# One more column in 128 fetched row by row on SyncE and ScalarE, and the passes written out

## The reference, cut to what matters

```python
def gcn_conv(x, src, dst, W, b, n_nodes):
    ...
    msg = h[src] * norm[:, None]
    out = jax.ops.segment_sum(msg, dst, num_segments=n_nodes)
    return out + b
def _edgeconv(x, src, dst, tw, tb, pw, pb):
    phi = x @ pw.T + pb
    diff = x[src] - x[dst]
    msg = diff @ tw.T + tb + phi[dst]
    agg = jax.ops.segment_max(msg, dst, num_segments=x.shape[0])
```

## Time and profile before

| | |
|---|---|
| median of 3 runs | 8914.77 us (8910.58 to 8919.87) |
| the profiled execution | 8913.79 us |
| its span, first to last instruction | 8912.1 us |
| PE busy | 7402.8 us (83%) |
| DVE busy | 5602.8 us (63%) |
| ACT busy | 823.6 us (9%) |
| POOL busy | 6615.4 us (74%) |

### The profile page before, as it was taken

How to read it: one execution, slowest core, us unless ns; L and a number is a source line. 1 busy time by engine, 2 the same in 40 slices (tenths; PEclk the granted TensorE clock), 3 DMA queues, 4 the chain that set the end, 5 groups by cost and what they waited for, 6 DMA issues and landing times. The chain is left out here.

```text
span 8912.1 us, 149042 instructions
## 1 busy us (share of the span) xinstructions
PE 7402.8 (83%) x34933; PEld 4053.7 (45%) x35458; DVE 5602.8 (63%) x11977; ACT 823.6 (9%) x2271; POOL 6615.4 (74%) x6356
## 2 busy tenths in 40 slices
PE   5999658887886899959997899959995899959994
PEld 2444347777775344434443344434443344434442
DVE  6777534444444777657775776757775776657775
ACT  3000011111113100010000100010001100010000
POOL 5777768888884677777777777777776777777777
PEclk8999867777777999979998999979997999979997
DMA  6555635555555333333333333333334333343334
GB/s 236 180 177 181 191 80 79 75 77 77 77 77 105 105 118 118 118 111 119 118 118 120 110 118 117 114 117 118 118 118 142 109 117 118 117 125 118 118 118 143
DMA packets 645241, 1072.25 MB, mean 120 GB/s; under 512 B 159799, under 2 KB 485007, under 8 KB 590297
## 3 DMA queue, kind: packets, MB, share of 16 engines
q0 software_dynamic: 295648, 412.64, 22.1%
q1 hardware_dynamic: 335527, 652.35, 21.3%
q10 hardware_dynamic: 13692, 3.78, 0.2%
HBM read 514.18 MB, written 562.58 MB: 121 GB/s over the span
## 5 line engine op out<-in xcount | busy, mean ns | idle before, releaser
L1056 POOL DMA_INDIRECT WORK<-table,stage x5040 | 4826.7, 958 | 1752.2 <-issue 1476.3
L1224 PE MATMUL bank<-TF,XF 128*128 128x512 bf16 x16800 | 5127.5, 386 | 485.8 <-DVE TF L1162 462.9
L1224 PE MATMUL bank<-TF,Z 128*128 128x512 bf16 x8400 | 3235.3, 385 | 4.8
L1224 PEld LDWEIGHTS bank<-TF,XF 128*128 128x128 bf16 x17150 | 1687.2, 99 | 2547.9 <-DVE TF L1162 329.5
L1162 DVE TENSOR_TENSOR TF<-AF,bank 128x3584 bf16<-128x3584 bf16 x1225 | 2470.7, 2017 | 314.0 <-PE bank L1224 308.2
L1189 DVE SCALAR_TENSOR_TENSOR WORK<-WORK,RESET 128x128 f32<-128x128 f32 x2928 | 1031.3, 352 | 892.4 <-DMA WORK<-table,stage 513.1
L1406 POOL DMA_INDIRECT acc<-TOT,stage x832 | 1296.0, 1558 | 275.7 <-issue 197.5
L1224 PEld LDWEIGHTS bank<-TF,Z 128*128 128x128 bf16 x8575 | 850.7, 99 | 1047.9 <-issue 64.2
L1189 DVE SCALAR_TENSOR_TENSOR WORK<-WORK,KEEP 128x128 f32<-128x128 f32 x2196 | 774.2, 353 | 663.2 <-DMA WORK<-table,stage 360.1
L1611 DVE SCALAR_TENSOR_TENSOR BASE<-bank,WEIGHT,BASE 128x128 f32<-128x128 f32 x832 | 234.3, 344 | 764.0 <-PE bank L1481 762.9
L1087 ACT COPY TOT<-bank 128x512 f32<-128x512 f32 x175 | 102.6, 586 | 5939.9 <-PE bank L1224 5539.5
(11 more groups left out here) (259 smaller groups left out, 3296.5 us busy)
## 6 DMA issues: line engine op xcount, KB each, us to landing
run_rows<-WORK SPq DMA_DIRECT2D x357, 1024.0 KB
WORK<-table ACTq DMA_DIRECT2D x5376, 0.5 KB
WORK<-table SPq DMA_DIRECT2D x5376, 0.5 KB
WORK<-table,stage POOLq DMA_INDIRECT x5040, 3.7
fill_rows<-BASE SPq DMA_DIRECT2D x52, 1024.0 KB
WORK<-fill_rows SPq DMA_DIRECT2D x104, 512.0 KB, 3.7
AF<-src_keys SPq DMA_DIRECT2D x175, 128.0 KB
table<-TF SPq DMA_DIRECT2D x56, 384.0 KB
```

Of the source, the lines that this page charges most:

```text
L1056: pool.indirect_dma_start(RUN[:, b, k, :], None, table, table_row(table, stage[:, b, k:k + 1]))\
L1224: i = nc.tensor.matmul(bank(2 + h)[:, 0:BATCH], PIECES[n][:, c * PART + k, :], OHOT[:, ((h + 1) * CHUNKS + c) % 2, k, :], start=c + k + n ...
```

## The change

`REGS` goes from 16 to 32: a part is one register load and 32 single rows, on both engines. `single(it, h)` says which columns come so: column 15 of the first half in rounds 1 to 12, as before, and now also column 15 of the second half (column 47) in odd rounds; GpSimd skips these. A column is four parts, two on SyncE and two on ScalarE. The semaphores and the row numbers are kept apart for the two halves. The registers are allocated once and not per pass. All `Fori` loops of a pass but TensorE's are replaced by Python loops, so that the code is written out and offsets and wait values are constants; `hold` becomes `wait`.

```diff
-SHARE = P // 2
-REGS = 16
+REGS = 32
+SHARE = 2 * REGS
...
+        def single(it, h):
+            return 0 < it < ROUNDS and (h == 0 or it % 2 == 1)
...
+            def alone(eng, regs, it, h, first, s):
+                if first % SHARE == 0:
+                    eng.wait_ge(solo_in[h], 16 * singles(it, h))
+                    eng.wait_ge(stored[2 * h], 16 * it)
+                    eng.wait_ge(reduced, (it - 1) * SPAN + h * COLS + HALF + 1)
+                eng.reg_load(regs, SOLO_I[0:1, h, first:first + REGS])
+                for k in range(REGS):
+                    row = eng.snap(regs[k], min_val=0, max_val=N_PAD - 1)
+                    eng.dma_start(RUN[first + k:first + k + 1, 2 * h, SOLO, :], table[ds(row, 1), :]).then_inc(s, 16)
...
-                        if (j % COLS >= OWN or j == SOLO) and not (first and j < COLS):
+                        if j % COLS >= OWN and not (first and j < COLS):
+                            continue
+                        if j % COLS == SOLO and single(it, j // COLS):
                             continue
...
# ScalarE, in each half round h after the copy and the indices:
-                        if not last:
-                            solo(it, h)
+                        if h == 0:
+                            solo(it, 1, 1)
+                            solo(it + 1, 0, 0)
+                        elif not last:
+                            solo(it + 1, 0, 1)
+                            solo(it + 1, 1, 0)
...
# SyncE, after the store of chunk b:
-                        if not last:
-                            solo(it, b)
+                        if b % 2 == 0:
+                            load_single(it + 1, b // 2)
+                        if b == 0:
+                            solo(it, 1, 1)
+                        else:
+                            solo(it + 1, b // 3, (b - 1) % 2)
...
# the same on SyncE, GpSimd and ScalarE:
-                body(0)
-                sp.addr_align(256, max_nops=8)
-                with sp.Fori(1, ROUNDS - 1) as it:
-                    body(it)
-                body(ROUNDS - 1, last=True)
+                for it in range(ROUNDS):
+                    body(it, last=it == ROUNDS - 1)
```

More of the change, by code:

```diff
@@ L313, in gnn_kernel @@
         added = [sem(f"added{k}", phase=False) for k in range(ACCS)]
+        regs_s = [nc.sync.alloc_register(f"row_sp{k}") for k in range(REGS)]
+        regs_a = [nc.scalar.alloc_register(f"row_act{k}") for k in range(REGS)]
         assert cleared[-1].num - cleared[0].num + 1 == len(cleared)
@@ L1012, in _, with singles @@
                     sp.wait_ge(x_saved, 16 * NG)
+        def single(it, h):
+            return 0 < it < ROUNDS and (h == 0 or it % 2 == 1)
+        def singles(it, h):
+            return sum(single(r, h) for r in range(it + 1))
         def turns(k):
             if k == SOLO:
-                return T // COLS - (ROUNDS - 1)
+                return T // COLS - sum(singles(ROUNDS - 1, h) for h in range(2))
             return T // COLS if k < OWN else 1
@@ L1076, in carry_clear @@
                     .then_inc(patched, 16)
-                hold(pool, patched, pbase + 32)
+                wait(pool, patched, pbase + 32)
             def act_part(act):
@@ L1081, in indices @@
                     wait(act, reduced, (c - BUFS + 1) * HALF)
[L1082 removed]
+                    act.copy(stage[:, b, :], SRCF[:, c * HALF:(c + 1) * HALF]).then_inc(staged, 1)
                 def rows_out(m, h):
@@ L1087, in rows_out, with solo @@
                     act.copy(TOT[:, h, 0:BATCH], bank(2 + h)[:, 0:BATCH]).then_inc(e_copied, 1)
[L1089 to L1099, removed]
+                def solo(it, h, part):
+                    if single(it, h):
+                        alone(act, regs_a, it, h, SHARE + part * REGS, solo_act[h])
                 def mixed(it, first=False, last=False):
@@ L1125, in act_part @@
                         i.then_inc(split_mid, 1)
[L1126 to L1131, removed]
+                solo(1, 0, 0)
+                for it in range(ROUNDS):
+                    mixed(it, first=it == 0, last=it == ROUNDS - 1)
             def dve_part(dve, st):
@@ L1247, in store @@
                 def store(c, b, first, n):
-                    hold(sp, reduced, c * HALF + first + n)
+                    wait(sp, reduced, c * HALF + first + n)
                     sp.dma_start(run_view[:, ds((c * HALF + first) * F, n * F)],
@@ L1253, in load_keys, with load_single, solo @@
                 def load_keys(m, h):
-                    hold(sp, onehot, (m - 2) * CHUNKS)
+                    wait(sp, onehot, (m - 2) * CHUNKS)
                     sp.dma_start(EKEYS_I[:, h, :], src_keys[ds((m * COLS + OWN) * P, BATCH)]
                                  .rearrange("(a n) -> a n", a=1).to_broadcast([P, BATCH])).then_inc(keys_in[h], 16)
[L1258 to L1270, removed]
+                def load_single(it, h):
+                    if single(it, h):
+                        sp.dma_start(SOLO_I[:, h, :], solo_rows[it * 2 + h:it * 2 + h + 1, :]).then_inc(solo_in[h], 16)
+                def solo(it, h, part):
+                    if single(it, h):
+                        alone(sp, regs_s, it, h, part * REGS, solo_sp[h])
                 def restore(g):
@@ L1284, in body @@
                         if fill:
-                            hold(sp, reduced, c * HALF + HALF // 2)
+                            wait(sp, reduced, c * HALF + HALF // 2)
                             sp.dma_start(fill_view[:, ds(c * HALF * F, HALF * F)], blank)\
@@ L1306, in sp_part @@
                     restore(0)
-                hold(sp, patched, pbase + 16)
+                wait(sp, patched, pbase + 16)
                 for g in range(NG):
```

32 lines of the change are left out of this document (13 added, 19 removed).

## The result

The changed kernel takes **9204.12 us** in the median of 4 runs (9198.03 to 9213.81); the kernel before, beside it, 8912.67 us (8906.75 to 8919.87). The ratio is 1.0327, with a 95% interval from 1.0315 to 1.0339. The forecast was 8862 us, in 8845 to 8900: the sign was wrong, and the distance is 342 us. The profiled execution took 9199.2 us, with a span of 9197.5.

What follows compares the result with a forecast made beforehand. POOL's gathers, at 1.263 us each, were taken to bound the kernel. 8913.8 us less 53.0 for 42 saved gathers gave 8860.8, or 8862 on the median, with everything else at nothing; range 8845 to 8900.

Steps and rivals of the forecast that it cites:

- the gathers saved: On POOL, 714 gathers a pass instead of 720, 42 fewer in seven passes at 1.263 us each: 53.0 us less.
- the code: Writing the loops out was costed at nothing, with bounds of 0 to 10 us either way.
- The loop: SyncE's and DVE's cycle over two rounds, closed by the late keys: 133.3 us, 4.4 shorter than POOL's 137.7.
- A part, 17.1 us: On SyncE, store, one register load and 32 single rows, 16.8 us, taken as 17.1; six stand in two rounds.
- the low end: A load of 32 registers was taken to cost no more than one of 16, so 0 us extra.
- The range's other end: Load of 32 registers in proportion: another 1.23 us, or another 2.87 if what stands behind the store doubled too.
- From the keys to the store, 30.7 us: Keys landing 2.5 us, then DVE's 28 columns at PE's pace, 28.2 us, to the store of chunk 1.
- rival 3: No change: PE's stalls and lowered clock at late keys make 139 us per two rounds, 8915 us in all; chance 0.06.
- The slack, 20 us: POOL has 27 gathers left on average, 34 us, against DVE's 14 us: about 20 us of lateness cost nothing.
- Rival 1: SyncE becomes the bound, slower: passes lengthen from 18.6 us per part; with 20.0, 52 us a pass, 9275; chance 0.12.
- the second: Rival: DVE and PE lateness just over the slack, up to 5 us of POOL wait a pass, 8880 to 8897; chance 0.11.
- the signs of being wrong: POOL waiting for DVE over 0.3 us, a load near 6 us, SyncE never idle through a pass, stores over a chunk late.

Runs made afterwards that it cites:

- the run meant for it: Changed kernel with 28 rows per part on SyncE and 36 on ScalarE, keys still behind the part: 9571.04 us, 1.0735 of the kernel before.
- the other: Changed kernel with SyncE's register load issued ahead of the chunk's store, keys still behind the single rows: 12404.28 us, 1.0124 of the kernel before.

## Why the prediction was wrong

**The bound, the gathers saved, the code.** Right. POOL bounded the passes, 42 gathers at the same beat are gone, and where nothing holds POOL up the pass lasts 902.4 us, as said. With the keys ahead and the first pass eased, which gives six of the 42 gathers back (7.6 us), the sum of the prediction is 8870 and the kernel takes 8868.47 (the kernel before took 8917.91 beside it, 3 more than in the sum); so the written-out code and the traffic together are worth some us at most, inside the 0 to 10 given for the code.

**The loop.** The mechanism was seen: the keys behind six parts are "what is late next". The ring was summed to 133.3 us, 4.4 under POOL's 137.7; it measured 145.6. The step that failed is this sum and the slack set against it. Three sizes in it were wrong:

- *A part, 17.1 us.* Six of them up to the late keys were put at 102.6 and took 110.9, 8.3 us of the 12.3. Most of that is the load of 32 registers, for which the prediction took "the low end", as for 16. Its line after, beside the earlier trace rows:

```profile
L1045 ACTq TENSOR_LOAD <-rowb x252: 2119/2143/6283, 187.6 to 9020.0; - x126
L1045 SPq TENSOR_LOAD <-rowb x252: 3797/4022/6429, 201.4 to 9036.9; - x126
```

  On ScalarE 2143 ns against 1292, so 53 ns for each further register; on SyncE behind a store 4022 against 2872, 1.15 us a part and 6.9 a ring. The argument "like one round trip and not like 16" was wrong: more registers take longer, though not in proportion. The range's other end had +1.23, which is nearly what came on SyncE. By itself it would not have turned the forecast: 133.3 + 6.9 = 140.2 is 2.5 over POOL's 137.7, 15 us in six double rounds, inside the 20 of slack that I set against it.
- *From the keys to the store, 30.7 us.* Measured 34.8 (3333.75 to 3368.52), the other 4.1. The landing is 3.3 us and not 2.5, and DVE's 28 columns take 31.5 and not 28.2. After the stop PE stands too, for 5.03 us, and only starts at 3339.14, once the first compare (2.02 us) is done. Then it starts slowly. By window (busy us of PE, PEld, DVE, ACT, POOL, then granted clock, DMA, GB/s):

```profile
3340.00:3345.00 5.00, 5.00 (x14) 1.82 (x13) 3.91 (x7) 0.00 (x0) 3.78 (x5) 0.55 0.18 51
3345.00:3350.00 5.00, 5.00 (x27) 2.55 (x26) 3.16 (x5) 0.00 (x0) 0.30 (x1) 1.00 0.04 15
```

  The granted clock was 1.00 until PE stood, 0.55 from 3340 to 3345 (near the lower of its two levels, 1.2 GHz), and 1.00 again after. Until 3344.2 three matmuls together took 1.28 us where they took 0.65 before the stop. DVE's third and fourth compare after the stop waited 2.17 and 1.29 us for PE, where the later ones wait 0.83 to 0.88. The prediction priced this clock only under rival 3, as PE's own time; it belongs in the ring, behind the late keys.
- *The slack, 20 us.* It is about 12.6. I counted the gathers that POOL has left on average. But the stop is at column 3 of a half round, and when POOL asks at the start of the next chunk, it has only this chunk's 12 gathers (15.1 us) less about 2.5 for the three columns. This figure is worked out afterwards, and no run varied it. The timeline shows POOL wait at such starts already in round 2, and again at the start of round 4:

```profile
3205.34 0.95 POOL L1074 DMA_INDIRECT WORK<-table,stage  x1 [2.04 <-DVE WORK L1200]
...
3311.28 0.95 POOL L1074 DMA_INDIRECT WORK<-table,stage  x1 [1.96 <-DVE WORK L1200]
```

With the three sizes in place the prediction's own formula works: six double rounds of 145.6 - 137.7 = 7.9 us are 47.4, less 12.6 of slack 34.8; the second pass is 937.5 - 902.4 = 35.1 over POOL's own, and passes 3 to 7 are 32 to 39 over it.

**The first pass.** "First-pass chunks have a fill DMA more" stood as a remark under the first rival, and the fill DMAs as a condition under the second; the sum had no term for them. SyncE's queue there:

```profile
377.34 0.43 SPq L1261 DMA_DIRECT2D run_rows<-WORK  x1
...
384.32 13.57 SPq L1048 DMA_DIRECT2D WORK<-table  x32
...
398.36 0.42 SPq L1294 DMA_DIRECT2D fill_rows<-BASE  x1
398.83 0.47 SPq L1261 DMA_DIRECT2D run_rows<-WORK  x1
405.98 13.60 SPq L1048 DMA_DIRECT2D WORK<-table  x32
```

Behind two large stores the first row leaves 6.7 us after the store's end (399.30 to 405.98), where it was 4.2 in the second pass (3223.21 to 3227.45); a part is 21.5 us here (377.34 to 398.83) where it was 18.55. This pass is 114.5 us longer than before.

**The rivals.** Rival 1, SyncE the bound and slower, is what happened. It said that a pass gets longer than before only from parts of 18.6 us on; they came at 18.55, and passes 2 to 7 were already 25 to 32 us longer, since it was worked out with the loop's other terms and the slack at my wrong values. So it seemed to need a load that grew more than in proportion, and got 0.12. That its 9275 is near 9204 is partly luck: it had parts of 20.0 us and 52 us in each pass alike. The forecast left 4.4 us between two rings of 133 and 138 us, with one uncertain term standing in the ring six times; such a gap gives no 0.68. The Trainium skill (Runtime: NRT & Kernel Launch, Instruction fetch mechanics) has about 200 ns per register; the rows show 53 ns for each further one on ScalarE and 72 on SyncE, so that size does not hold for these loads, which read an on-chip tile (`rowb`). That the load grows with its registers does hold. Rival 3 (PE's stalls add up to POOL's old time) is refuted in its terms: the time went far past 8915. Of the signs of being wrong that the prediction named, the trace shows a POOL wait for DVE over 0.3 us, and an SP without idle time, if not through a pass then for six chunks of eight; a load near 6 us did not come.

**Left open:** how the excess divides between the parts' length and the keys' place on a chip of 8.9 ms, since the run meant for it made ScalarE late and the other fell on a 12.24 ms chip; whether the first pass had too many parts or too much traffic; and ScalarE's own margin.

## What to carry to other kernels

When work is added to a queue, follow the small transfer that stands behind it to whoever waits for it, and close the ring: sum every term of one turn, and where the bound's margin is a few per cent, take every unseen price at its high end together and not one at a time, since a price inside the ring counts as often as it stands there. A stop inside the ring also costs what the stopped engines need to get going again. Issue what another engine waits for ahead of what nobody waits for yet; here moving each keys DMA ahead of 32 single rows was worth 308 us. Slack is read at the one instant at which the stop falls, not as a mean, and a pass that carries an extra transfer is its own stage with its own sum.

## What the runs showed of the hardware that was not expected

- A register load of 32 took 2.14 us on ScalarE and, on a chip of 12.24 ms, 1.73 us on SyncE ahead of a store; behind one store it took 4.0, and behind fill and store the rows started after 6.7 us. A load on ScalarE that began within 2 us of a store on SyncE took 3.5 to 4.0 us too.
- On three chips the kernel before took 12.24 to 12.34 ms instead of 8.92, and there single rows are issued slower, while a gather on POOL takes 955 to 960 ns as elsewhere. A register operation ahead of a row (L1047) took 44 to 64 ns in the changed kernel on its chip, and with keys ahead on one of those chips up to 1531 ns, at the same median of 44. SyncE's queue with keys ahead on such a chip, 26.96 us for 32 rows against 13.6:

```profile
337.14 26.96 SPq L1048 DMA_DIRECT2D WORK<-table  x32
```

  Versions of one kernel stand differently there (two columns only: 1.044 to 1.046 against 1.007; keys ahead with TensorE's rounds written out and the load ahead: 1.0012). What makes those chips slow was not found.
